# Fifteen decode steps in slots of their own, Wo prepared at other slots, and a narrower store of values

## The chip, the cores and the metric

One NeuronCore of one Trainium2 chip runs the kernel. It has five queues that work at once: TensorE (PE; its weight loads are shown as PEld), VectorE (DVE), ScalarE (ACT), GpSimd (POOL) and SyncE (SP), which only issues DMAs. The metric is the time of one execution on the device in microseconds; lower is better. A profile is taken of one execution, and shows each instruction with its start, its length and what ended the idle time before it.

## The reference

A transformer block over 2048 tokens of width 512, whose attention and MLP both read the same normalised input:

```
xn  = layernorm(x)                                  # [2048, 512]
q, k, v: 16 query heads, 4 key/value heads, 32 wide # Wq, Wkv
scores = q k^T / sqrt(32) + slope * (key - query)   # causal, ALiBi
attn = softmax(scores) v  ->  @ Wo + bo
W = LUT[4-bit codes] * scales, blocks of 32         # gate, up: 4096x512, down: 512x4096
mlp = down( gelu_tanh(gate(xn)) * up(xn) )
out = x + attn + mlp
```

The result is wanted close to float32. So most matrix products are made of fp16 pairs: an operand is split into a high and a low part, and three matmuls (high by high, high by low, low by high) stand for one.

## The kernel before, in words

A preamble (the first 112 us) normalises x, turns it, projects q, k and v and stores them in DRAM, and makes the scales and the first group's weights. Then come 16 groups; group i does the attention of head i and the MLP for hidden units 256 i to 256 i + 255, with all 2048 tokens. A tail adds x and the output projection.

**Slots.** A group has 48 slots, and each queue walks through them with its own program: in each slot TensorE does one piece of the MLP (six matmuls of gate, up or down, `PIECES`), and, where the table `PLAN` says so, one block of scores (a 128-row tile of queries by up to 512 keys, line 1370) and one unit of attention by values (line 1394). Heads begin 8 slots before their group. What an engine does in a slot is written out by hand in its `body`; an engine takes its instructions strictly in this order, waits for semaphores, and may so be some slots behind TensorE.

- TensorE: scores into a ring of four PSUM banks; gate and up; down, whose bank VectorE must have added to `acc` (line 1545) first.
- VectorE: maximum of each score block (1588, 1590), the shift for the softmax (1609), two steps of gelu (1554, 1561), the product with up (1569), its cast to fp16 (1577), the accumulation (1545), and the decoding.
- ScalarE: the exponentials (1475), their cast to the high fp16 half (1485, into a ring of four `pair` buffers, each free when its transpose has landed), square and tanh of gelu (1456, 1462), and `rows_hi` (389).
- GpSimd: low half of the probabilities (1734), low half of the MLP's product, `il` (1742), and `rows_lo` (393).
- SyncE: transposes of the probabilities by DMA (`turn`, 1203), q and k loads, gathering and storing of outputs, transposes of the weights (`turn_rows`, 399), and loads of the packed weights (`load_raw`, 352 and 357).

**Decoding the next weights.** While group i runs, the weights of group i + 1 are made, for the matrices m = 0, 1, 2 (gate, up, down), each in five instructions on VectorE (`decode_step`): shift the low code into place (366), the high code (369), mask both (373), and scale each half into `wf` (382, twice). One step stands in a slot: the rows of five begin at slots 8, 18 and 28 (`DECODE_FROM`). At the row's start + 5 ScalarE writes the fp16 high rows over the raw buffer, at + 6 GpSimd the low rows into a part of `o3`, at + 8 SyncE issues the two transposes, at + 11 the load of the raw weights of group i + 2 into the same buffer, which waits until the transposes have landed. The last group decodes nothing.

**Wo, in the last group (15).** `load_early` (SyncE, slot 12) brings Wo into the buffers of the decoding, by four DMAs, and a row of scales by a fifth. `wo_max` (VectorE, slots 17 to 20) takes its maxima and minima per partition, two reductions in each slot; `spread_tops` (SyncE, slot 27) writes the 128 maxima to DRAM, waits for that, and reads them back to all partitions; `wo_scale` (VectorE, slot 29) waits for it and makes the scale; ScalarE casts the high parts in slots 31 to 34 and VectorE makes the low parts a slot later. `load_x` (slot 41) waits for them.

**Values.** In the preamble, v is split into a high and a low half; the tile `vt` has four parts of 32 columns per head: high, ones, low, zeros. GpSimd fills ones and zeros by two memsets. `store_values` writes all four parts to `v_parts` in DRAM. At slot 0 of groups 0, 4, 8 and 12 `load_v` (1168) brings the high and the low part in with two DMAs, in runs of 64 bytes.

## Time and profile before

| | |
|---|---|
| median of 3 runs | 1640.24 us (1639.86 to 1642.94) |
| the profiled execution's own time | 1641.02 us |
| its span, first to last instruction | 1639.2 us |
| busy: TensorE / VectorE | 1429.3 us (87%) / 1297.4 us (79%) |
| busy: ScalarE / GpSimd | 975.9 us (60%) / 1000.8 us (61%) |
| mean granted TensorE clock | 0.977 |
| DMA queue of SyncE, share of 16 engines' span | 80.8% |

The busy times are shares of the whole span, preamble and tail included. In rows of a timeline the first number is the start in us from the span's start, the second the length; in square brackets stands how long the engine was idle before, and what ended that. A row of a timeline can merge several instructions (x4). `L382` is line 382 of the kernel. Matmul ends are modelled, so TensorE's idle time is a little less than what a stop costs.

### The profile page before, as it was taken

What the parts mean: (1) busy time and instruction counts of PE and PEld (TensorE: products, weight loads), DVE (VectorE), ACT (ScalarE), POOL (GpSimd) and SP (SyncE); (2) the same over time, 40 slices, a digit from 0 to 9 for tenths busy, and PEclk for the clock granted to TensorE, in tenths of its full rate; (3) what the DMA queues carried; (4) which work ended last, traced back from release to release, by engine and by line L of the source; (5) the groups of instructions that cost most, each with busy time, mean ns of one, the idle gap of its engine ahead of it and who ended that gap; (6) DMA issues with size and microseconds to landing.
All of it is one profiled execution on the core that took longest, in us unless ns stands there. A gap on an engine that the chain in (4) does not pass through costs nothing.

```text
span 1639.2 us, 28993 instructions
## 1 busy us (share of the span) xinstructions
PE 1429.3 (87%) x9281; PEld 684.1 (42%) x9281; DVE 1297.4 (79%) x2639; ACT 975.9 (60%) x2124; POOL 1000.8 (61%) x670
## 2 busy tenths in 40 slices
PE   5978998999889989889989989899888999897598
PEld 4743443444334434444434434344433444343243
DVE  8858787888868788888868788888868788875466
ACT  3347666666656666665666666666656666664330
POOL 3226676666656677666656666777656766774341
PEclk9979999999999999999999999999999999998799
DMA  7878969788897888798889879886998988887665
GB/s 219 231 176 175 171 119 170 149 161 154 160 163 144 160 155 165 145 152 149 166 158 153 157 151 160 147 174 136 173 154 154 153 158 153 147 152 133 120 155 198
DMA packets 784799, 260.97 MB, mean 159 GB/s; under 512 B 734512, under 2 KB 755896, under 8 KB 784392
## 3 DMA queue, kind: packets, MB, share of 16 engines
q1 hardware_dynamic: 780328, 253.48, 80.8%
q10 hardware_dynamic: 4320, 5.64, 1.0%
q8 instruction: 75, 1.23, 0.3%
q14 instruction: 76, 0.62, 0.1%
HBM read 52.30 MB, written 21.89 MB: 45 GB/s over the span
## 4 chain that ended last, share of the span: by engine, by line
DVE 30%; PE 18%; issue 14%; ACT 10%; DMA 10%; POOL 6%; SPq 4%; ACTq 0%; DVEq 0%; POOLq 0%
DMA pt<-pair 8%; PE up_ps L1348 5%; ACT p L1475 5%; POOL pair L1734 5%; DVE mxp L1588 4%; DVE acc L1545 4%; PE gate_ps L1348 4%; PE s_ps L1370 3%; DVE dec L369 3%; DVE wf L382 3%; DVE prod L1569 2%; PE down_ps L1326 2%; ACT gl L1456 2%; DVE s_ps L1590 2%; DVE dec L373 2%
## 5 line engine op out<-in xcount | busy, mean ns | idle before, releaser
L1734 POOL TENSOR_TENSOR pair<-p,pair 128x1024 f16<-128x1024 f32 (+7 forms) x384 | 615.2, 1610 | 347.3 <-ACT pair L1485 344.9
L1475 ACT ACTIVATE p<-s_ps,shift 128x512 f32<-128x512 f32 (+3 forms) x640 | 393.2, 619 | 222.6 <-DVE shift L1609 220.9
L1370 PE MATMUL s_ps<-kst,qst 128*128 128x512 f32 (+3 forms) x640 | 344.7, 540 | 115.2 <-ACT p L1475 106.9
L1485 ACT ACTIVATE pair<-p 128x1024 f16<-128x1024 f32 (+7 forms) x384 | 308.3, 808 | 100.4 <-DMA pt<-pair 97.3
L1588 DVE TENSOR_REDUCE mxp<-s_ps 128x1 f32<-128x512 f32 x384 | 260.2, 683 | 103.5 <-PE s_ps L1370 101.5
L1742 POOL TENSOR_TENSOR il<-prod,ih 128x512 f16<-128x512 f32 x128 | 156.2, 1220 | 149.7 <-DVE ih L1577 149.7
L1370 PEld LDWEIGHTS s_ps<-kst,qst 128*128 128x128 f32 x640 | 123.2, 193 | 233.6 <-ACT p L1475 157.9
L1326 PE MATMUL down_ps<-wh,ih 128*128 128x512 f16 x506 | 195.9, 387 | 28.2 <-DVE acc L1545 28.2
L1326 PE MATMUL down_ps<-wh,il 128*128 128x512 f16 x506 | 193.0, 381 | 16.0 <-POOL il L1742 16.0
L1348 PE MATMUL up_ps<-xh,wh 128*128 128x512 f16 x512 | 200.2, 391 | 0.0
L1348 PE MATMUL gate_ps<-xh,wh 128*128 128x512 f16 x512 | 197.6, 386 | 0.6 <-DVE gl L1561 0.6
L1348 PE MATMUL up_ps<-xh,wl 128*128 128x512 f16 x512 | 197.2, 385 | 0.0
L1348 PE MATMUL up_ps<-xl,wh 128*128 128x512 f16 x512 | 196.7, 384 | 0.0
L1348 PE MATMUL gate_ps<-xh,wl 128*128 128x512 f16 x512 | 194.7, 380 | 0.0
L1348 PE MATMUL gate_ps<-xl,wh 128*128 128x512 f16 x512 | 194.6, 380 | 0.0
L1326 PE MATMUL down_ps<-wl,ih 128*128 128x512 f16 x506 | 193.1, 382 | 0.0
L1545 DVE TENSOR_TENSOR acc<-down_ps,acc 128x512 f32<-128x512 f32 x237 | 161.3, 681 | 24.6 <-PE down_ps L1326 24.4
L1590 DVE CUSTOM_DVE_ANT_0 s_ps<-s_ps,mask_row 128x128 f32<-128x128 f32 (+3 forms) x256 | 125.5, 490 | 29.4 <-PE s_ps L1370 29.0
L1554 DVE SCALAR_TENSOR_TENSOR gl<-gl,gate_ps 128x512 f32<-128x512 f32 x128 | 87.5, 684 | 69.9 <-ACT gl L1456 66.5
L1394 PE MATMUL o_ps<-pt,vst 128*32 128x256 f16 (+1 forms) x3456 | 119.2, 272 | 27.0 <-DMA pt<-pair 17.0
L1456 ACT ACTIVATE gl<-gate_ps,cur 128x512 f32<-128x512 f32 x128 | 87.2, 682 | 69.3 <-PE gate_ps L1348 69.2
L1475 ACT ACTIVATION_READ_ACCUMULATOR p<-s_ps,shift 128x1 f32 x640 | 128.2, 200 | 0.0
(249 smaller groups left out, 2064.6 us busy)
## 6 DMA issues: line engine op xcount, KB each, us to landing
o<-oraw SPq DMA_DIRECT2D x256, 64.0 KB, 2.0
qst<-q_parts SPq DMA_DIRECT2D x192, 64.0 KB
q_parts<-o SPq DMA_DIRECT2D x24, 256.0 KB, 3.4
pt<-pair SPq DMA_TRANSPOSE x384, 4.3
raw<-L_ffn_gate_W_packed_dram SPq DMA_DIRECT2D x16, 256.0 KB, 3.1
raw<-n_L_ffn_up_W_packed_dram SPq DMA_DIRECT2D x16, 256.0 KB, 3.0
raw<-L_ffn_down_W_packed_dram SPq DMA_DIRECT2D x32, 128.0 KB, 2.6
o<-l_recips SPq DMA_DIRECT2D x64, 64.0 KB, 2.1
```

The lines of the kernel that those rows point to most:

```text
L1326: mm = nc.tensor.matmul(dst[:], lhs, rhs, start=(q == 0), stop=(q == 5))
L1348: mm = nc.tensor.matmul(dst[:], lhs, rhs, start=(q == 0), stop=(q == 11))
L1370: nc.tensor.matmul(s_ring[n % len(s_ring)][:, 0:cols], qst[:, c % 2, i4 * P:(i4 + 1) * P], kst[:, m * CH:m * CH + cols], start=True, stop= ...
L1394: mm = nc.tensor.matmul(dst if tok else dst.rearrange("p (a n) -> p a n", a=2), lhs, rhs, start=k < VPARTS, stop=k + VPARTS >= len(todo), ...
L1456: nc.scalar.activation(gl[a][:], gate_ps[:], ACT.Square, scale=cur[par][:, a:a + 1]).then_inc(square_done, 1)
L1475: nc.scalar.activation(p32[p % PR][:, at:at + cols], s_ring[n % len(s_ring)][:, 0:cols], ACT.Exp, bias=shift[t % len(shift)][:, 0:1], accu ...
L1485: nc.scalar.activation(pair[n % PH][:, 0:cols], p32[n % PR][:, 0:cols], ACT.Copy).then_inc(phi_done, 1)
L1545: nc.vector.tensor_tensor(acc[:, n % NT, :], bank[:], before, ALU.add).then_inc(acc_done, 1)
L1588: nc.vector.tensor_reduce(mxp[t % 2][:, m:m + 1], bank[:, 0:cols], AX.X, ALU.max).then_inc(red_done, 1)
L1590: nc.vector.tensor_tensor_reduce(bank[:, 0:cols], bank[:, 0:cols], mask_row[:, CH - cols:CH], 1.0, -3e38, ALU.add, ALU.max, mxp[t % 2][:, ...
L1734: nc.gpsimd.tensor_tensor(pair[n % PH][:, cols:2 * cols], p32[n % PR][:, 0:cols], pair[n % PH][:, 0:cols], ALU.subtract).then_inc(plo_done, 1)
L1742: nc.gpsimd.tensor_tensor(il[w % 2][:, a, :], prod[a][:], ih[w % 2][:, a, :], ALU.subtract).then_inc(il_done, 1)
```

## The change

Three things are changed; the arithmetic of the result is not.

1. The decode steps get slots one by one, listed for each matrix; what follows them keeps its distance from the last step (+ 1, + 2, + 4, + 7, as before).
2. In the last group, the load of Wo goes from slot 12 to slot 1, the maxima from 17 to 20 to 14, 16, 17 and 19; `spread_tops` is split into `store_tops` (slot 21) and the reading back (slot 28); the scale goes from 29 to 37, the casts from 31 to 34 to 38, 40, 42 and 43, the load of x from 41 to 46.
3. `vt` and `v_parts` have two parts for four; the memsets and the wait for them go, and `load_v` is one DMA. The first `load_raw(0, 1)` is issued ahead of the last store of values, not in slot 0.

```diff
-DECODE_FROM = (8, 18, 28)
-DECODE_AT = {s + step: (m, step) for m, s in enumerate(DECODE_FROM) for step in range(5)}
-ROWS_HI_AT = {s + 5: m for m, s in enumerate(DECODE_FROM)}
-ROWS_LO_AT = {s + 6: m for m, s in enumerate(DECODE_FROM)}
-TURN_ROWS_AT = {s + 8: m for m, s in enumerate(DECODE_FROM)}
-LOAD_RAW_AT = {s + 11: m for m, s in enumerate(DECODE_FROM)}
+DECODE_SLOTS = ((4, 7, 10, 13, 14), (16, 19, 22, 24, 25), (28, 31, 32, 34, 37))
+DECODE_AT = {s: (m, step) for m, slots in enumerate(DECODE_SLOTS) for step, s in enumerate(slots)}
+SCALES_READY_AT = DECODE_SLOTS[0][0]
+ROWS_HI_AT = {slots[-1] + 1: m for m, slots in enumerate(DECODE_SLOTS)}
+ROWS_LO_AT = {slots[-1] + 2: m for m, slots in enumerate(DECODE_SLOTS)}
+TURN_ROWS_AT = {slots[-1] + 4: m for m, slots in enumerate(DECODE_SLOTS)}
+LOAD_RAW_AT = {slots[-1] + 7: m for m, slots in enumerate(DECODE_SLOTS)}
-LOAD_EARLY_AT, LOAD_FULL_AT, SPREAD_TOPS_AT, LOAD_X_AT = 12, 25, 27, 41
+LOAD_EARLY_AT, LOAD_FULL_AT, STORE_TOPS_AT, SPREAD_TOPS_AT, LOAD_X_AT = 1, 25, 21, 28, 46
-WO_MAX_AT, WO_SCALE_AT, WO_HI_AT = (17, 18, 19, 20), 29, (31, 32, 33, 34)
+WO_MAX_AT, WO_SCALE_AT, WO_HI_AT = (14, 16, 17, 19), 37, (38, 40, 42, 43)
...
-    v_s = nc.dram_tensor("v_parts", [KVH, P, NT, 4 * HD], F16, kind="Internal").ap()
+    v_s = nc.dram_tensor("v_parts", [KVH, P, NT, 2 * HD], F16, kind="Internal").ap()
...
-                nc.gpsimd.memset(vt[:, :, :, 1, :], 1.0).then_inc(vt_filled, 1)
-                nc.gpsimd.memset(vt[:, :, :, 3, :], 0.0).then_inc(vt_filled, 1)
...
-                    for part in range(2):
-                        sp.dma_start(vst[:, :, part * HD:(part + 1) * HD],
-                                     v_s[i // REP, :, :, 2 * part * HD:(2 * part + 1) * HD]).then_inc(v_in, 16)
+                    sp.dma_start(vst[:], v_s[i // REP]).then_inc(v_in, 16)
...
+                sp.wait_ge(w_in[0], 16 * W_DMAS)
+                load_raw(sp, 0, 1)
                 store_values(sp, NCH - 1)
...
-                    for m in range(3):
+                    for m in (1, 2):
...
-                def spread_tops():
+                def store_tops():
 
                     sp.wait_ge(wtop_done, 1)
                     sp.dma_start(w_s.rearrange("(p o) -> p o", o=1), wtop).then_inc(wtop_out, 16)
+
+                def spread_tops():
+
                     sp.wait_ge(wtop_out, 16)
...
-                        if s == DECODE_FROM[0]:
+                        if s == SCALES_READY_AT:
```

## Rows read from the trace of the kernel before

**Rows 1.** Stretches: busy us (x instructions) of each engine, granted clock, DMA share, GB/s.

```profile
658.30:690.70 32.40, 28.59 (x181) 12.59 (x179) 25.64 (x53) 20.55 (x46) 22.50 (x15) 1.00 0.82 145
1470.60:1498.40 27.80, 27.80 (x181) 12.60 (x179) 21.24 (x49) 21.04 (x48) 19.19 (x14) 1.00 0.77 135
1212.40:1215.70 3.30, 3.30 (x9) 1.11 (x7) 1.20 (x3) 0.00 (x0) 1.27 (x1) 0.52 0.86 162
296.60:1470.60 1174.00, 1051.94 (x7089) 483.75 (x7087) 963.30 (x1964) 758.27 (x1664) 791.83 (x522) 0.99 0.85 155
```

**Rows 2.** TensorE's waits, groups 2 to 14: us in total, times, longest.

```profile
PE s_ps L1370 <- ACT p L1475: 87.6, 80, 2.0
PE down_ps L1326 <- POOL il L1742: 13.7, 13, 1.1
PE o_ps L1394 <- DMA vst<-v_parts: 9.8, 3, 3.6
```

**Rows 3.** Timeline of TensorE in group 6: start, length in us, [idle before, releaser].

```profile
680.53 0.49 PE L1370 MATMUL s_ps<-kst,qst 128*128 128x512 f32 x1 [0.84 <-ACT p L1475]
...
689.22 0.49 PE L1370 MATMUL s_ps<-kst,qst 128*128 128x512 f32 x1 [1.69 <-ACT p L1475]
...
694.65 0.51 PE L1370 MATMUL s_ps<-kst,qst 128*128 128x512 f32 x1 [0.54 <-ACT p L1475]
...
703.29 0.49 PE L1370 MATMUL s_ps<-kst,qst 128*128 128x512 f32 x1 [1.59 <-ACT p L1475]
...
721.46 0.50 PE L1370 MATMUL s_ps<-kst,qst 128*128 128x512 f32 x1 [1.49 <-ACT p L1475]
```

**Rows 4.** Timeline of VectorE in group 6.

```profile
683.99 2.54 DVE L382 TENSOR_TENSOR wf<-dec,sc 128x512 f32<-128x512 f16 x1
```

**Rows 5.** Timeline of ScalarE in group 6.

```profile
686.57 1.06 ACT L389 ACTIVATE raw<-wf 128x1024 f16<-128x1024 f32 x1 [4.01 <-DVE wf L382]
```

**Rows 6.** Timeline of VectorE in group 15.

```profile
1513.79 0.69 DVE L1661 TENSOR_REDUCE sc<-wf 128x1 f32<-128x512 f32 x1 [12.15 <-DMA dec<-in_L_attn_Wo_dram]
...
1553.18 0.29 DVE L1671 TENSOR_REDUCE sc<-sc 128x1 f32<-128x128 f32 x1 [16.16 <-DMA sc<-wo_tops]
```

**Rows 7.** Timeline of SyncE's issues in group 15.

```profile
1499.78 1.30 SPq L1285 DMA_DIRECT2D wf<-in_L_attn_Wo_dram  x2
```

**Rows 8.** DMA issues, groups 2 to 14: count, KB each, median us to landing.

```profile
raw<-L_ffn_gate_W_packed_dram SPq DMA_DIRECT2D x12, 256.0 KB, 3.1
...
vst<-v_parts SPq DMA_DIRECT2D x6, 128.0 KB, 4.2
```

**Rows 9.** VectorE's decode instructions, groups 2 to 14: busy us, mean ns | idle before.

```profile
L382 DVE TENSOR_TENSOR wf<-dec,sc 128x512 f32<-128x512 f16 x78 | 78.5, 1020 | 0.0
...
L373 DVE TENSOR_SCALAR dec<-dec 128x1024 int32<-128x1024 int32 x39 | 48.2, 1237 | 0.0
L369 DVE TENSOR_SCALAR dec<-raw 128x512 int32<-128x512 int32 x39 | 42.2, 1082 | 0.0
...
L366 DVE TENSOR_SCALAR dec<-raw 128x512 int32<-128x512 int32 x39 | 28.9, 742 | 0.0
```

**Rows 10.** Timeline of SyncE's issues in group 6.

```profile
663.49 1.36 SPq L1203 DMA_TRANSPOSE pt<-pair  x1
...
715.61 1.32 SPq L399 DMA_TRANSPOSE wl<-o  x1
718.51 0.40 SPq L352 DMA_DIRECT2D raw<-n_L_ffn_up_W_packed_dram  x1
...
732.00 1.58 SPq L399 DMA_TRANSPOSE wh<-raw  x1
733.63 1.33 SPq L399 DMA_TRANSPOSE wl<-o  x1
...
738.73 0.94 SPq L357 DMA_DIRECT2D raw<-L_ffn_down_W_packed_dram  x2
```

**Rows 11.** Chain of waits, the longest pieces of 660 to 760: start, us.

```profile
746.16 4.11 DMA pt<-pair
```

More of the change, by code:

```diff
@@ L408, in storing_steps @@
         e[n] for n in ("q_s", "k_s", "aug_s", "qst", "kst", "p_out", "q_in", "k_in", "k_last"))
-    vt = wh[1][:, 0:2].rearrange("p m a n -> p (m a n)").rearrange("p (j g a d) -> p j g a d", j=TPC, g=KVH, a=4)
+    vt = wh[1][:, 0].rearrange("p a n -> p (a n)").rearrange("p (j g a d) -> p j g a d", j=TPC, g=KVH, a=2)
     orows = acc[:, NT - 1, OROWS_AT:OROWS_AT + P]
@@ L539, in preamble @@
         vscale_done = sem("vscale_done")
-        vt_filled = sem("vt_filled")
         os_turned = sem("os_turned")
@@ L572, in store_v @@
                     sp.wait_ge(v_lo, c + 1)
-                    if c == 0:
-                        sp.wait_ge(vt_filled, 2)
                     store_values(sp, c)
@@ L921, in values_lo @@
                     nc.vector.scalar_tensor_tensor(
-                        vt[:, :, :, 2, :].rearrange("p j g d -> p (j g) d"), vps[:].rearrange("p (n d) -> p n d", d=HD),
+                        vt[:, :, :, 1, :].rearrange("p j g d -> p (j g) d"), vps[:].rearrange("p (n d) -> p n d", d=HD),
                         vscale[:, 0:1], vt[:, :, :, 0, :].rearrange("p j g d -> p (j g) d"), ALU.mult, ALU.subtract
@@ L1245, in body @@
                                 load_full(sp, 0)
+                            if s == STORE_TOPS_AT:
+                                store_tops()
                             if s == SPREAD_TOPS_AT:
@@ L1376, in values @@
                         if u == 0:
-                            pe.wait_ge(v_in, (h // REP + 1) * 32)
+                            pe.wait_ge(v_in, (h // REP + 1) * 16)
                         for n in range(max(last - PH + 1, 0), last + 1):
```

## The prediction

> **What bounds the kernel now.** I read the page's first two parts, then the chain of waits, the waits of TensorE, the timelines of one head group, and the last group by itself. The page puts TensorE at 87% busy, VectorE at 79%. A group (one head of attention beside one sixteenth of the MLP, 48 slots) takes 90.3 us: 1174 us for groups 2 to 14, thirteen of them [rows 1]. No engine is full, so what counts is what stops TensorE. Over those thirteen groups it waited 87.6 us for exponentials on ScalarE, 13.7 us for `il` from GpSimd and 9.8 us for the values, three times [rows 2].
>
> Where the waits for exponentials fall is seen in group 6: 0.84 and 1.69 us behind the first row of decode steps (slots 8 to 12), 0.54 and 1.59 behind the second, 1.49 behind the third [rows 3]. The chain there: the fifth step of the first row took 2.54 us on VectorE [rows 4] at a place where the scores' maxima were due; ScalarE stood 4.01 us before the copy to fp16 rows that needs this step [rows 5], with a gelu square and the next exponentials queued behind; then TensorE found no free score bank. The third row's rows_lo on GpSimd (slot 34) delays `il`, needed at slot 38.
>
> The last group is the control: it decodes nothing. Its first 17 slots are the same 181 matmuls as in group 6, in 27.8 us with TensorE busy throughout, against 32.4 us [rows 1]. Its later part is worse: VectorE stood 12.15 us for Wo and 16.16 us for the broadcast of Wo's maxima [rows 6], and TensorE behind it, since accumulate and the score maxima share that queue.
>
> **Part 1, Wo in group 15.** The load now leaves at SyncE's slot 1, the first maximum is taken at slot 14; before, slots 12 and 17. SyncE runs behind the others there: slot 12's load was issued at 1499.78 [rows 7], when VectorE was already at slot 17, and landed at 1513.8 (the row of 12.15 us). From slot 1, issued near 1480, it should land near 1494, and slot 14 starts at 1494. That wait shrinks to 0 to 3 us. The broadcast gets nine slots (28 to 37) in place of two, some 15 us, its store leaves seven slots ahead of it: that wait goes. 12.15 + 16.16 = 28.3. After each of the two stops TensorE ran some 3 us at half its clock, near 2 us more each: 32 us. Against it: the five DMAs take 5 us of the queue (from 1499.78, [rows 7], to 1504.7) ahead of the transposes of probabilities, in a stretch where it has nothing to spare. It can cost TensorE 0 to 5; I take 2. The Wo reductions and casts are the same instructions; in 38 to 44 the casts stand before the last pairs on ScalarE, but the present 2.75 us wait at slot 47, which has the same source, is caused at 31 to 34; I leave it equal. `load_x(0)` at 46 stays behind the same transposes. Gain 30 (20 to 35).
>
> **Part 2, values.** One load of 256 KB in 2 KB runs for two of 128 KB in 64 B runs, and a smaller store. TensorE waited 9.8 us for it over groups 4, 8 and 12 [rows 2], and each wait is followed, as in group 12, by 3.3 us at granted clock 0.52 (1.2 GHz) for nine matmuls, some 1.3 us lost [rows 1]. The second load was issued 0.7 to 1.4 us after the first and landed 4.2 us later; a 256 KB load of raw weights lands in 3.1 us [rows 8]. So the wait falls by some 2 us, and part of the slow clock goes: 3 us each, 9 in all (3 to 14). The two memsets dropped from GpSimd stood ahead of a wait for ScalarE's first cast: nothing. The early `load_raw(0, 1)` puts one issue (0.6 us) ahead of the last store of values, and load_v gives one back: nothing, within 1 us either side.
>
> **Part 3, the decode steps, groups 0 to 14.** What the rows cost: in group 6, 0.84 + 1.69, 0.54 + 1.59, 1.49 plus 1.05 (13.7 over 13) for `il`, 7.2 us of idle; six stops, and each loses about 0.24 us more, since idle is counted from a matmul's modelled end and not from where the next would have started. 8.6 us. The comparison of 32.4 with 27.8 agrees: 4.6, of which the wait at slot 2, not from decode, and its restart are some 1.5.
>
> No instruction is added or dropped: per matrix 0.742 + 1.082 + 1.237 + 2 x 1.020 = 5.1 us [rows 9], 15.3 per group, now in slots where VectorE has little else (7, 13, 22, 37 have almost nothing). VectorE is then never five slots in arrears: its lag behind TensorE, up to 6.0 us at slots 12, 15 and 21 now, should stay under 4.5, where I find no stop now. But slots 10 to 19 hold about as much VectorE work as TensorE work (16 us each), so what remains of a lag doesn't drain there. I take two thirds of the 8.6: 5.7. Bounds: nothing, and all of it.
>
> What is moved with them: rows_hi, rows_lo, the transposes and the next raw load go from slots 13, 14, 16, 19 to 15, 16, 18, 21; from 23, 24, 26, 29 to 26, 27, 29, 32; from 33, 34, 36, 39 to 38, 39, 41, 44. On GpSimd the third rows_lo (2.1 us) leaves the place ahead of `il`, and comes behind the last pairs of the head and before `il` of slot 41, needed only at slot 2: hidden. On ScalarE it joins output_hi at 38, one us, and 40 is empty. SyncE is the tight one. From 663.49 to 753.09 in group 6 (76 issues, the first in [rows 10]) it was issuing or stepping between issues in all but 7 of 90 us, so a group can't fall below some 84 us unless the issues get shorter. The third matrix's two transposes (1.58 + 1.33) and its raw load (0.94) [rows 10] now come after the transposes of the head's last pairs, which helps slot 47 a little, and amid the first ones of the next head. Its raw load must wait for transposes that left just before: as the second's does now, 716.9 to 718.51, 1.6 us [rows 10]; between 41 and 44 there is only the store of outputs and one transpose. The turns of slots 45 to 47 go some 2.5 us later, that of 44 by 0.8. That place is on the chain of waits: 4.11 us at 746.16 [rows 11]. Cost 0.8 to 5.5 (all three issues and the wait); I take 1.5, since the turn of 44 is the one on the chain. Net 4.2 per group, x 15 = 63 us. Bounds: -1.5 x 15 and, by the SyncE floor of 84, 6.3 x 15 = 95.
>
> **Sum.** The profiled execution took 1641.0 us, 1.8 outside its span of 1639.2. 1641.0 - 30 - 9 - 63 = 1539. The median of the runs is 0.8 below it: 1538.
>
> **A rule that speaks against part 3.** The fifth step took 2.54 us where the mean of its kind is 1.02 [rows 4, 9], and the time lies inside the instruction. The Trainium skill (SBUF — State Buffer, on the shared port pair) says that VectorE instructions with two SBUF inputs or in a two-port mode, and GpSimd instructions, take one lock for their whole length, and the other blocks fully. The trace agrees as far as one row can. If fifteen lone steps each meet a GpSimd instruction, every one pays, and spreading buys nothing; this is the second rival, priced below from rows.
>
> **Rivals.**
> (a) SyncE keeps pace and nearly all decode stops go: 6.3 to 8.6 per group. 1641 - 39 - 95 = 1507, at the end 1480. For: in group 15 without decode there was no stop at all in 17 slots. Against: there rows and raw loads were absent from SyncE as well.
> (b) The stops only move, through long steps in new places: 15 x 0 to 15 x 1.5 gained. 1602 to 1580, say 1595. VectorE is at 963.3 / 13 = 74 us of 90 per group [rows 1]; three more long steps (1.5 us over the mean each) make 78.6, still under the group, so it would cost the gain and no more. For: fewer steps in a row means more meetings. Against: GpSimd was as busy before, 792 of 1174 us [rows 1].
> (c) Slower than before: the wrap from slot 41 to slot 2. If the three issues and the wait, 1.58 + 1.33 + 0.94 + 1.6 = 5.5 us, land in full on the first transposes of the next head, ScalarE's ring of four pairs stops exponentials at slots 47 to 2 every group. It is decided at 39 / 15 = 2.6 us per group over the decode gain: with a gain of 1.5 and a cost of 5.5, 1641 - 39 + 15 x 4 = 1662. For: the chain passes there already. Against: no turn but slot 44's is on it, and that one goes ahead of the raw load.
> (d) It doesn't do what it says: VectorE's slots are not light because its lag carries over from before; the time is that of (b).
>
> **Chances.** Forecast (1515 to 1570) 0.53, (a) 0.17, (b) with (d) 0.22, (c) 0.06, no change 0.02. The range, 1505 to 1600, takes in the bounds of parts 1 and 2, most of (b) and the near end of (a). This kernel's runs tell 0.2%, some 3 us, from no change. Faster 0.92, same 0.02, slower 0.06.
>
> **What would show it.** Group 15 near 88 us in place of 117, VectorE's waits for Wo and `wo_tops` under 3 us; `vst` waits near 1 us each; groups of 86 us; waits at slots 12, 16, 19, 23, 33 mostly gone, `il` no longer a releaser of down; the wait at slot 2 grown to about 3 us; SyncE idle under 3 us per group. Wrong would be: new waits for exponentials at slots 17 to 26 or 35 to 41, or groups still over 89 us.

## The result

| | before | after |
|---|---|---|
| median | 1638.97 us (1635.6 to 1644.05, 19 runs) | 1629.88 us (1627.09 to 1640.63, 19 runs) |
| ratio | | 0.995, 95% interval 0.9937 to 0.9962 |
| span of the profiled execution | 1639.2 us | 1626.6 us |
| groups 0 to 14, mean of one | 90.56 us | 90.56 us |
| group 15 | 117.6 us | 103.6 us |
| preamble / tail | 112.1 / 51.0 us | 114.7 / 49.9 us |

Faster by 0.4 to 0.6%, some 8 us, where 1538 us with a range of 1505 to 1600 was predicted (6%). The fifteen groups that decode are as long as before, to the hundredth; all that was gained lies in the last. (A group's length is the distance between the first matmuls of two groups, in the profiled execution.)

The page of the kernel after, busy us of each engine:

```profile
PE 1443.6 (89%) x9281; PEld 693.7 (43%) x9281; DVE 1273.6 (78%) x2639; ACT 978.3 (60%) x2124; POOL 1018.7 (63%) x668
```

Stretches of the kernel after, groups 2 to 14 and group 15; the columns are those of [rows 1]:

```profile
296.60:1473.10 1176.50, 1064.93 (x7087) 492.17 (x7086) 937.24 (x1964) 760.81 (x1664) 809.02 (x520) 0.98 0.81 155
1473.10:1576.70 103.60, 83.70 (x540) 38.04 (x539) 66.02 (x140) 54.06 (x114) 51.65 (x34) 0.92 0.80 146
```

TensorE's waits in the kernel after, groups 2 to 14, as in [rows 2]:

```profile
PE s_ps L1371 <- ACT p L1476: 71.0, 64, 3.4
PE o_ps L1395 <- DMA pt<-pair: 22.1, 16, 2.4
PE gate_ps L1349 <- DVE gl L1562: 12.8, 11, 1.4
PE o_ps L1395 <- DMA vst<-v_parts: 5.5, 3, 2.5
```

The waits for exponentials fell by 16.6 us only, `il` is gone and the values cost half. But transposes that came late grew from 7.3 to 22.1 us, and the second gelu step (12.8 us, none before) is new. The longest wait for exponentials grew from 2.0 to 3.4 us: fewer waits, longer ones. The clock took a share as well: in groups 2 to 14 the same matmuls kept TensorE busy for 1064.9 us at a granted clock of 0.98, against 1051.9 at 0.99 in [rows 1], one us more per group. A large piece lies behind the stops of slot 28, here in group 6 (columns as in [rows 1]):

```profile
711.00:714.00 3.00, 2.90 (x41) 1.68 (x42) 0.04 (x1) 1.44 (x2) 1.29 (x1) 0.73 1.33 164
```

TensorE in group 6 (657.1 to 748.3 us) of the kernel after, to be held against [rows 3]:

```profile
662.61 0.50 PE L1371 MATMUL s_ps<-kst,qst 128*128 128x512 f32 x1 [2.14 <-ACT p L1476]
...
682.60 0.81 PE L1395 MATMUL o_ps<-pt,vst 128*32 128x256 f16 x24 [0.82 <-DMA pt<-pair]
...
707.85 0.50 PE L1371 MATMUL s_ps<-kst,qst 128*128 128x512 f32 x1 [1.48 <-ACT p L1476]
...
711.10 1.14 PE L1395 MATMUL o_ps<-pt,vst 128*32 128x256 f16 x36 [2.08 <-DMA pt<-pair]
...
736.71 0.39 PE L1349 MATMUL gate_ps<-xh,wh 128*128 128x512 f16 x1 [1.36 <-DVE gl L1562]
...
745.45 0.39 PE L1371 MATMUL s_ps<-kst,qst 128*128 128x256 f32 x1 [1.27 <-ACT p L1476]
```

The stops of [rows 3] are gone; these stand at slots 2, 13, 28 (two), 42 and 47. Counted over groups 2 to 14, as the excess of the distance between two matmuls over what it is where nothing waits (this is my sum over TensorE's records, not a view; it takes in matmuls at the slow clock, and another choice of the distance without a wait moves a row by some tenths, the sums by some 2 us), per group. "The wrap" is the passage from the last slots of a group to the first of the next:

| stop at slot | before, us | after, us | what ends it |
|---|---|---|---|
| 12, 16, 19, 23, 33, 38 | 8.62 | 1.41 | VectorE behind a row of decode steps |
| 28, 29: values, up, down | 0 | 3.05 | a transpose that landed late |
| 28: scores | 0.55 | 1.83 | exponentials behind a late tanh |
| 2: scores, down | 1.18 | 2.86 | exponentials; the wrap |
| 42: gate | 0 | 1.12 | gelu, ScalarE |
| 47: scores and values | 0.57 | 1.58 | exponentials |
| all stops | 12.56 | 12.98 | |

So the mechanism of part 3 did what was said of it, 7.2 us per group (5.7 predicted); and 7.6 us came in other places. The places of the largest are seen in group 6.

**SyncE, slots 21 to 28.** Its issues in the kernel after:

```profile
704.32 1.86 SPq L1199 DMA_TRANSPOSE pt<-pair  x1
706.22 1.06 SPq L353 DMA_DIRECT2D raw<-L_ffn_gate_W_packed_dram  x1
707.34 5.66 SPq L1199 DMA_TRANSPOSE pt<-pair  x3
```

The transpose issued at 707.34 is the one whose values TensorE needs at slot 28; it lands at 710.97 (3.63 us on the chain), and TensorE goes on at 711.10. It wasn't the data that was late: over groups 2 to 14 this transpose's input lay ready 6.9 us before the issue, 5.6 in the kernel before (these and the next are my medians over the records of GpSimd, SyncE and TensorE). The load of the first matrix's raw weights, 1.06 us, stands ahead of it on the queue, but it did so in the kernel before too:

```profile
700.10 0.58 SPq L352 DMA_DIRECT2D raw<-L_ffn_gate_W_packed_dram  x1
700.73 0.36 SPq L1178 DMA_DIRECT2D qst<-aug_rows  x1
701.14 1.23 SPq L1180 DMA_DIRECT2D qst<-q_parts  x3
702.47 3.89 SPq L1203 DMA_TRANSPOSE pt<-pair  x2
```

Two things are new. SyncE is late from the wrap on, where the third matrix's issues now stand: counted from the group's start, the transpose of slot 3 is issued at 12.2 us for 9.7 before, and that of slot 22, the one in question, at 50.2 for 47.5. (At slots 17 and 18 it is level with before for a moment, as the first matrix's two transposes now stand behind these and not ahead.) And TensorE comes to slot 28 sooner, at 50.9 us for 52.5. Before, the transpose landed at 51.0, ahead of TensorE; now it lands at 54.1, three us behind.

**VectorE and ScalarE, slots 25 to 28.** VectorE in the kernel after:

```profile
702.21 0.68 DVE L383 TENSOR_TENSOR wf<-dec,sc 128x512 f32<-128x512 f16 x1
...
703.41 2.02 DVE L383 TENSOR_TENSOR wf<-dec,sc 128x512 f32<-128x512 f16 x1
...
705.70 0.68 DVE L1555 SCALAR_TENSOR_TENSOR gl<-gl,gate_ps 128x512 f32<-128x512 f32 x1
```

ScalarE there:

```profile
705.47 1.06 ACT L390 ACTIVATE raw<-wf 128x1024 f16<-128x1024 f32 x1 [1.09 <-DVE wf L383]
706.43 0.71 ACT L1463 ACTIVATE gl<-gl,cur 128x512 f32<-128x512 f32 x1
707.04 0.67 ACT L1476 ACTIVATE p<-s_ps,shift 128x512 f32<-128x512 f32 x1
```

The second matrix's fifth step takes 2.02 us in slot 25. The gelu step behind it, then the tanh on ScalarE, then the exponentials stand in one line, and TensorE waits for these until 707.85. There are two suspects in that line: the decode step, and the high row (L390) that waits for it.

Why the step is long is in the trace. GpSimd's instruction that was running when it began:

```profile
702.30 2.58 POOL L1735 TENSOR_TENSOR pair<-p,pair 128x1024 f16<-128x1024 f32 x1
```

It ends at 704.88, the step 0.55 us later. So does every long one: of the 78 scaling steps of groups 2 to 14, 37 took over 0.9 us, all 37 began while a GpSimd instruction ran, and all ended 0.55 to 0.56 us after its end. In the kernel before there were 13 long ones, by the same rule. The change made nearly three times as many.

**GpSimd, slots 38 to 42** in the kernel after (L335 is the output's low part, L394 the third matrix's low row):

```profile
737.49 1.17 POOL L335 TENSOR_TENSOR o<-o 128x512 f16<-128x512 f32 x1
738.60 2.33 POOL L1735 TENSOR_TENSOR pair<-p,pair 128x1024 f16<-128x1024 f32 x1
740.89 2.13 POOL L394 TENSOR_TENSOR o<-wf,raw 128x1024 f16<-128x1024 f32 x1
742.99 1.15 POOL L1743 TENSOR_TENSOR il<-prod,ih 128x512 f16<-128x512 f32 x1
```

The change put the third matrix's rows at 38 and 39, where the output's steps stood already. The same meeting is on ScalarE. The rows are read here as the suspects for slots 42 and 47; e6 and e11 below try it.

**Group 15.** VectorE's list of waits there names neither Wo nor the maxima any more. In their place, on SyncE of the kernel after:

```profile
1483.96 1.26 SPq L1283 DMA_DIRECT2D wf<-in_L_attn_Wo_dram  x2
1485.27 1.33 SPq L1283 DMA_DIRECT2D dec<-in_L_attn_Wo_dram  x2
1486.64 2.42 SPq L1284 DMA_DIRECT2D raw<-column_scales  x1
1489.18 10.47 SPq L1199 DMA_TRANSPOSE pt<-pair  x2
```

And on TensorE:

```profile
1500.36 1.15 PE L1395 MATMUL o_ps<-pt,vst 128*32 128x256 f16 x18 [9.52 <-DMA pt<-pair]
```

SyncE's record of two transposes lasts 10.47 us right behind Wo's load, where that of two at 695.93 in group 6 lasts 3.74, and TensorE stands 9.52 us for them.

### The profile page after: what moved, and what is told of

It reads as the page before. It is cut to its first block, busy times and chain, and to the rows that moved or that the text cites. A ratio compares the mean times of both kernels' runs of the same rounds, so it can differ in the third digit from the quotient of the medians.

```text
span 1626.6 us, 28986 instructions
## 1 busy us (share of the span) xinstructions
PE 1443.6 (89%) x9281; PEld 693.7 (43%) x9281; DVE 1273.6 (78%) x2639; ACT 978.3 (60%) x2124; POOL 1018.7 (63%) x668
## 4 chain that ended last, share of the span: by engine, by line
PE 25%; DVE 20%; POOL 14%; issue 13%; DMA 9%; ACT 8%; SPq 4%; ACTq 0%; DVEq 0%; POOLq 0%
POOL pair L1735 10%; DMA pt<-pair 8%; PE up_ps L1349 6%; PE gate_ps L1349 5%; PE down_ps L1327 5%; DVE mxp L1589 5%; DVE acc L1546 3%; PE o_ps L1395 3%; ACT p L1476 3%; PE s_ps L1371 3%; POOL il L1743 2%; DVE prod L1570 2%; SPq L1199 2%; DVE s_ps L1591 2%; DVE wf L383 2%
## 5 line engine op out<-in xcount | busy, mean ns | idle before, releaser
L1735 POOL TENSOR_TENSOR pair<-p,pair 128x1024 f16<-128x1024 f32 (+7 forms) x384 | 640.2, 1678 | 325.2 <-ACT pair L1486 324.9
L1349 PE MATMUL gate_ps<-xh,wh 128*128 128x512 f16 x512 | 197.4, 386 | 12.8 <-DVE gl L1562 12.8
L1395 PE MATMUL o_ps<-pt,vst 128*32 128x256 f16 (+1 forms) x3456 | 126.3, 283 | 48.6 <-DMA pt<-pair 42.8
L1562 DVE SCALAR_TENSOR_TENSOR gl<-gl,gate_ps 128x512 f32<-128x512 f32 x128 | 87.3, 682 | 66.2 <-ACT gl L1463 65.8
L1555 DVE SCALAR_TENSOR_TENSOR gl<-gl,gate_ps 128x512 f32<-128x512 f32 x128 | 87.3, 682 | 65.2 <-ACT gl L1457 63.4
```

What stands on the lines that cost most here:

```text
L1349: mm = nc.tensor.matmul(dst[:], lhs, rhs, start=(q == 0), stop=(q == 11))
L1395: mm = nc.tensor.matmul(dst if tok else dst.rearrange("p (a n) -> p a n", a=2), lhs, rhs, start=k < VPARTS, stop=k + VPARTS >= len(todo), ...
L1555: nc.vector.scalar_tensor_tensor(gl[a][:], gl[a][:], 1.0, gate_ps[:], ALU.add, ALU.mult).then_inc(inner_done, 1)
L1735: nc.gpsimd.tensor_tensor(pair[n % PH][:, cols:2 * cols], p32[n % PR][:, 0:cols], pair[n % PH][:, 0:cols], ALU.subtract).then_inc(plo_done, 1)
```

## The experiments

Medians are of 4 to 9 runs each; the kernel before, run beside them, gave medians of 1636 to 1639 us. Theory S: SyncE's queue of issues. Theory P: the pile-up of the output's and the third matrix's rows. Theory D: Wo's bytes on the DMA engines. Theory Q: the decode step of slot 25. Where an expectation gives one of these letters another sense, it says so.

### Each part alone: e1, e2, e10

Each is the kernel before with one part of the diff shown ahead of the prediction: e1 with the lines from `DECODE_SLOTS` to `LOAD_RAW_AT`, e2 with the Wo slots and `store_tops`, e10 with the narrow values and the moved first load. The first line of each:

```diff
 # e1
+DECODE_SLOTS = ((4, 7, 10, 13, 14), (16, 19, 22, 24, 25), (28, 31, 32, 34, 37))
 # e2
+WO_MAX_AT, WO_SCALE_AT, WO_HI_AT = (14, 16, 17, 19), 37, (38, 40, 42, 43)
 # e10
+    v_s = nc.dram_tensor("v_parts", [KVH, P, NT, 2 * HD], F16, kind="Internal").ap()
```

> The kernel before with part 3 alone: the fifteen decode steps and what follows them in the new slots. Theory S (SyncE's queue is the floor of a group: the decode stops went, and the same microseconds came back as waits for transposes and pair buffers): groups stay at 90.6 us within 0.7, waits of TensorE for exponentials at slots 12, 16, 23, 33 gone, new ones at 28, 42 and 47; 1639 within 8. Theory V (part 3 gained its 60 us and the two other parts lost it): groups near 87 us, 1585.

> The kernel before with part 1 alone: Wo's load at slot 1, maxima, scale and casts at the new slots. Theory S: group 15 has its two stops of 12 and 16 us no more, but the five DMAs put ahead of the transposes stop TensorE some 10 us near slot 9; group 15 from 117 to about 104 us, whole 1626 (-13). My forecast of before said 2 us for that stop and -30: 1609.

> The kernel before and the values' part of the change alone (values without their constant columns, one load each, the first raw load moved). The prediction gave this part 9 us: 1628 to 1632 us. Theory S (SyncE's queue holds the stream by the group's sum of issues, and the values' loads save one issue in four groups): almost nothing of it comes through, 1634 to 1640 us; the waits for the values fall from 9.8 to about 5 us, and come back elsewhere.

| | median us | ratio to before | 95% interval | in us |
|---|---|---|---|---|
| e1, decode slots | 1653.63 | 1.0101 | 1.0071 to 1.0131 | +17 |
| e2, Wo | 1627.46 | 0.9933 | 0.9904 to 0.9961 | -11 |
| e10, values | 1628.59 | 0.9943 | 0.992 to 0.9965 | -9 |
| all three | 1629.88 | 0.995 | 0.9937 to 0.9962 | -8 |

(The last column is the ratio minus 1, times 1639.) The parts add up to -3, with intervals of 4 to 5 us on each: with the whole they agree. Values brought what was predicted, 9 (6 to 13), and theory S's own expectation for it, next to nothing, failed. Wo brought 11 for 30. The decode slots by themselves made the kernel slower, for 63 faster. In e1's trace groups 0 to 14 take 91.3 us each, 0.7 more than before, 11 us in sum; another 3 us lie in the preamble, which e1 doesn't touch.

### SyncE relieved: e3 and e5

```diff
+ACT_STORE_RECIPS_AT, ACT_SPREAD_RECIPS_AT = 6, 17
+ACT_RAW_AT = {25: (0, 2), 36: (1, 2), 10: (2, 1)}
...
-                            if s in LOAD_RAW_AT and i + 2 < HEADS:
...
+                        if s in ACT_RAW_AT and i >= 0:
+                            m, ahead = ACT_RAW_AT[s]
...
+                                load_raw(act, m, g)
```

The DMAs of raw weights (four) and of reciprocals (eight), twelve of some 77 a group, leave from ScalarE instead of SyncE, with the waits that stood before them, and in other slots; the bytes are the same. (e5's expectation counts six and six; it is four and eight.) e3 does it to the changed kernel, e5 to the kernel before.

> The changed kernel, with 12 of SyncE's 76 issues per group (raw weight loads, storing and spreading of the reciprocals) issued from ScalarE's queue in slots where it has little (6, 10, 17, 25, 36). Same DMAs, same bytes. Theory S: SyncE gets some 6 us back per group, the waits at slots 2 and 28 shrink by over half, groups fall by 3 us or more: 1585 or less. Rival D (the DMA engines themselves, 85% busy, are the floor, not the issuing): transposes land as late as now, groups within 1 us of 90.6, 1630. Rival P (GpSimd and ScalarE at slots 38 and 39 set it): waits at 42 and 47 stay, groups fall by 1 to 2 us at most.

> The kernel before, and of SyncE's issues twelve a group (six loads of raw rows, six stores and spreads of reciprocals) made by ScalarE instead; decode rows, Wo and values as before. It asks whether the relief needs the new slots. Theory S (two limits lie one behind the other: with the rows of five the decode clusters hold back the stream, with single slots SyncE's queue does): the clusters still stop TensorE at slots 16, 23 and 33, SyncE is less late than there, little comes back: 1625 to 1640 us, the stops before the block and values matmuls that name a transpose's DMA going but no more than 1 us per group. Rival (SyncE's queue alone set the group's length, whatever the slots): the group shortens by some 2.7 us as it did with the single slots, and the time is 1590 to 1600 us.

e3: 1584.83 us, ratio 0.9685 (0.9658 to 0.9711), 45 us under the changed kernel. The late transposes of slot 28 are gone. TensorE's waits of e3, groups 2 to 14:

```profile
PE s_ps L1365 <- ACT p L1470: 69.5, 65, 3.1
PE gate_ps L1343 <- DVE gl L1566: 15.0, 13, 1.4
PE o_ps L1389 <- DMA vst<-v_parts: 2.1, 3, 1.2
PE o_ps L1389 <- DMA pt<-pair: 1.8, 2, 1.0
```

`pt<-pair` went from 22.1 to 1.8 us and the two rows that theory S does not speak of stayed. The sum of SyncE's issue records went from 78.4 to 72.6 us per group, the group from 90.5 to 87.7. The same bytes alone don't rule the DMA engines out, since e3 also moves the twelve DMAs in time. The transposes' own records do: from a transpose's input being ready to its issue it took 3.2 us in the kernel after and 1.5 in e3, from its issue to its landing 4.1 and 4.3 (my means over the 312 transposes of groups 2 to 14). The time was lost ahead of the issue, in the queue, and not in the engines. Whether fewer issues or fewer waits in the queue brought more is not separated.

e5: 1614.38 us, ratio 0.9867 (0.9845 to 0.9889), 22 us under before, between the two expectations. So SyncE cost the kernel before some 20 us too, which TensorE's waits for transposes (7.3 us) had not shown; with the single slots it cost twice that. The stops at 16, 23 and 33 are in e5 what they were (2.02, 1.94, 1.84 us per group).

### The output's steps apart from the third rows: e6 and e11

```diff
-OUTPUT_HI_AT, OUTPUT_LO_AT = 38, 39
+OUTPUT_HI_AT, OUTPUT_LO_AT = 36, 37
```

> The changed kernel with ScalarE's twelve issues as in e3, and the output's high and low steps at slots 36 and 37 instead of 38 and 39. Theory P (the stops at slots 42 and 47, 1.3 and 1.6 us per group in e3, come of output_hi, rows_hi, the power and the exponential all lying in slot 38 on ScalarE, and output_lo, rows_lo in 39 on GpSimd): both stops shrink to under 0.5 us, the group from 87.85 to 85.5 to 86.5 us, and the time is 1550 to 1565 us. Rival D (the stops come of the block's own work at those slots, or of DMA traffic): nothing moves, 1582 to 1588 us.

> The changed kernel, and the output's high and low steps at slots 36 and 37 instead of 38 and 39, with all twelve issues still on SyncE. Behind the relief the same edit took 31 us (e3 to e6). If the group's length is SyncE's queue (theory S), the stops at 42 and 47 go here too, but their time comes back as longer waits for the transposes: 1615 to 1630 us. If the two limits only add up, each with its own price, it is 1595 to 1602 us.

e6: 1553.82 us, ratio 0.9498 (0.9479 to 0.9516), 31 us under e3. The stop at 47 went from 1.61 us per group to 0, that at 42 from 1.31 to 0.73, that at 2 from 2.51 to 1.88; one of 1.11 came at 44, where down waits for VectorE. TensorE's waits of e6, groups 2 to 14:

```profile
PE s_ps L1365 <- ACT p L1470: 44.3, 52, 2.3
PE down_ps L1321 <- DVE acc L1550: 12.3, 13, 1.0
PE gate_ps L1343 <- DVE gl L1566: 7.6, 12, 0.8
```

e11, the same edit with all issues on SyncE: 1610.74 us, ratio 0.9836 (0.9809 to 0.9862), 19 us under the changed kernel, more than theory S allowed and less than the 31 us behind the relief. The late transposes stayed (21.1 us for 22.1). So each of the two limits has a price of its own, 45 and 19 us, and together they bring 76, 12 more than the sum.

### What the decode slots are worth then: e13

> The kernel before with both of e6's additions (ScalarE's twelve issues, output steps at 36 and 37), but rows of five, Wo and values as before. It measures what the decode slots are worth where nothing else is late. If the prediction's mechanism was right and only its gain was eaten by the two limits, this kernel stays near e5, at 1608 to 1622 us, since the stops at 16, 23 and 33 are still VectorE's clusters; e6 is then some 60 us faster, of which 21 are Wo and values as measured alone, and the rest, 35 to 40 us, is the decode slots' (predicted: 63). Rival (the gain of e6 is the relief's and the output's own, whatever the slots): 1575 to 1585 us.

1610.01 us, ratio 0.9825 (0.9806 to 0.9843). With rows of five, both additions brought 29 us; with single slots 76. TensorE's waits of the whole e13:

```profile
PE s_ps L1364 <- ACT p L1469: 98.7, 91, 3.5
PE down_ps L1320 <- DVE acc L1549: 23.5, 3, 13.9
PE down_ps L1320 <- POOL il L1746: 16.9, 15, 1.1
```

The stops at 16, 23 and 33, behind the rows of five, are there as in [rows 3], 2.0, 1.8 and 1.8 us per group. e6 against e13 is a ratio of 0.9498 / 0.9825 = 0.967, 54 us; less the 20 of Wo and values, 34 for the decode slots, with some 7 either way from the intervals of the four ratios. By the same sum their worth is 10 us with SyncE relieved alone (0.9685 / 0.9867: 30 less 20, some 8 either way), and -17 with nothing relieved (5 either way). This is the main finding: one edit, three prices, by what stands behind it. That the prices of Wo and values are the same in all three settings is taken over, not measured. The lengths of groups 0 to 14 in the traces, in which Wo has no part, say the same: less the 12.6 us that values bring there in e10, the decode slots are worth -11 us (e1), 9 (89.30 in e5, 87.85 in e3) and 31 (89.00 in e13, 86.09 in e6).

### The stop at slot 28: e7, e9, e12

```diff
 # e7: the rows wait some slots
-ROWS_HI_AT = {slots[-1] + 1: m for m, slots in enumerate(DECODE_SLOTS)}
+ROWS_HI_AT = {15: 0, 30: 1, 40: 2}
 # e9
-DECODE_SLOTS = ((4, 7, 10, 13, 14), (16, 19, 22, 24, 25), (28, 31, 32, 34, 37))
+DECODE_SLOTS = ((4, 7, 10, 13, 14), (16, 19, 20, 22, 24), (28, 31, 32, 34, 37))
 # e12
+DECODE_SLOTS = ((4, 7, 10, 13, 14), (16, 19, 22, 24, 28), (31, 32, 34, 37, 39))
```

> As e6, and each matrix's row steps wait a few slots after its last decode step (high 15, 30, 40; low 16, 31, 42; turn 18, 33, 44), so that the high row's step on ScalarE isn't held by a decode step just ahead of it. Theory P: the stop of 1.83 us before the block matmuls of slot 28 (there ScalarE's power waits behind the high row of slot 26, which waits for VectorE's long decode step of slot 25) goes to under 0.6 us, and the wrap's stop at slot 2 (2.5 us) to under 1.5 us, since the third row is done within the group: 2 us per group less than e6, 1520 to 1540 us. Rival (the stop at 28 is the decode step itself on VectorE, not the row behind it): within 5 us of e6.

> As e6, and the second matrix's decode steps at slots 16, 19, 20, 22 and 24 instead of 16, 19, 22, 24 and 25. In e7 the row steps were taken away from slot 26 and the stop before slot 28's block matmuls stayed 1.82 us. Theory Q (the stop comes of the decode step itself: in slot 25 it lasts 2 us on VectorE, the gate's inner step of slot 26 starts behind it, ScalarE's tanh of slot 27 waits for that, the two exponentials wait behind the tanh, and the block matmuls of slot 28 for the exponentials): the stop falls to 0.5 to 0.8 us, 1.1 us per group, 1534 to 1543 us. Rival (the other work of slots 24 to 26 holds it, or a decode step at slot 20 takes its place): the time stays at 1550 to 1556 us, or a new stop of the same size shows at slots 21 to 24.

> As e6, and the second matrix's last decode step at slot 28 instead of 25, the third's five at 31, 32, 34, 37 and 39 instead of 28, 31, 32, 34 and 37 (in e6's trace VectorE idles 1.5 us in slot 28 and 1.1 in slot 39). Theory Q (the step in slot 25 makes the stop at slot 28, and e9 lost its gain only to the steps packed at 20 and 22): the stop at slot 28 falls from 1.83 to about 0.5 us, nothing new of that size comes, 16 us per run less than e6: 1532 to 1542 us. Rival (VectorE is so full from slot 16 to 37 that any place of the fifteen steps costs the same): a stop moves to slot 31, 33 or 42, 1550 to 1560 us.

e7, e9 and e12 all stand on e6. e7: 1561.6 us, ratio 0.955 (0.9533 to 0.9566), 8 us slower than e6. The stop at 28 stayed at 1.82 us per group with the row out of the way, so it was not the row. The stop at 2 went from 1.88 to 0.63, and 0.6 and 0.99 came at 4 and 9: nothing won.

e9: 1588.59 us, ratio 0.9692 (0.9665 to 0.9719). The stop at 28 fell to 0.89, so it was the decode step; but 2.76 and 0.66 us came at slots 23 and 24, behind the steps packed at 20 and 22, and the kernel is 32 us slower than e6 by the ratios. Moving three decode steps by one or two slots each cost four times what the whole change had won.

e12: 1552.28 us, ratio 0.9472 (0.945 to 0.9494), the fastest, though not told apart from e6. TensorE of e12 at slot 28 of group 6:

```profile
680.91 0.49 PE L1365 MATMUL s_ps<-kst,qst 128*128 128x512 f32 x1 [0.20 <-ACT p L1470]
```

VectorE of e12 just before:

```profile
678.14 0.43 DVE L1595 CUSTOM_DVE_ANT_0 s_ps<-s_ps,mask_row 128x256 f32<-128x256 f32 x1 [0.31 <-PE s_ps L1365]
```

The stop there is 0.55 in place of 1.83, as theory Q had it, and VectorE even waits for work. Of the 16 us per run expected from that, 1.5 came: the stop at 42 (0.73) went as well, but those at 2, 3, 4, 9 and 28 (values) grew by 1.7 us per group in sum, and all stops went from 7.77 to 7.50.

### Wo: e4, e8, e14

e4 issues Wo's five DMAs from ScalarE at slot 3. e8 is e7 with Wo's four loads at slots 43 and 47 of group 14 and at 3 and 8 of group 15. e14 is the changed kernel with half of Wo's bytes: it leaves out the load of Wo's last 256 columns, so their part of the result is not computed from Wo.

```diff
 # e4, on ScalarE
+                        if i == LAST and s == 3:
+                            load_early(act)
 # e8, per (group, slot): which part of Wo, the last the row of scales
+WO_LOADS = {(LAST - 1, 43): 2, (LAST - 1, 47): 3, (LAST, 3): 0, (LAST, 8): 1, (LAST, 28): KVH}
 # e14
-sp.dma_start(wo[g], Wo.rearrange("(r g d) n -> g r d n", r=REP, g=KVH)[g]).then_inc(wo_in, 16)
+sp.dma_start(wo[g][:, 0:C // 2], Wo.rearrange("(r g d) n -> g r d n", r=REP, g=KVH)[g][:, :, 0:C // 2]).then_inc(wo_in, 16)
```

> The changed kernel, with the five DMAs of Wo's load issued by ScalarE at slot 3 of group 15 and not by SyncE at slot 1. Theory Q (they held the transposes because they stood ahead in the same queue): the 10 us stop near slot 9 is 0 to 3 us, 1622. Rival D (1.25 MB ahead of the transposes in the DMA engines, whoever issues): a stop of 6 to 10 us stays, 1629.

> As e7, and Wo's four loads spread out on SyncE: two in the last slots of group 14 (43, 47), two in group 15 (slots 3 and 8), the column at slot 28. Theory D (the stop of 10 us at slot 9 of the last group is the transposes' DMAs queued behind Wo's 1.25 MB on the DMA engines, so it shrinks when they never lie together): the stop falls to under 4 us, the time is 6 to 9 us under e7. Rival: the loads, wherever they lie, delay the transposes by the same sum, and the time is within 2 us of e7.

> The changed kernel, but Wo's four loads at slot 1 bring the first 256 of 512 columns alone (0.5 MB instead of 1 MB; the other half of Wo isn't computed with the right numbers). Theory D (the transposes' DMAs share the DMA engines with the load's bytes): the stop before slot 9's values matmuls falls from 10.3 to 5 to 6 us, 4 to 5 us less in the run than the changed kernel's 1629.9. Rival (a transpose issued behind five bulk copies pays a fixed price, a drain or a change of mode, whatever their size): the stop stays at 9.5 us or more, and so does the time.

e4: 1629.74 us, ratio 0.9951 (0.992 to 0.9981), the changed kernel's. Stops of 3.6, 1.3 and 4.7 us at slots 6, 7 and 9 for one of 10.3. SyncE of e4, while Wo's loads are issued by ScalarE from 1487.3 to 1493.4:

```profile
1489.88 14.32 SPq L1209 DMA_TRANSPOSE pt<-pair  x2
```

No load of Wo is ahead of these two on SyncE's queue. Of the 14.32 us some 1.6 are a wait for the second's input; the two issues themselves last 4.92 and 7.81 us, and the first transpose lands 16.3 us after its issue (10.9 in the kernel after, 4.4 at 695.93 in group 6).

e8: 1560.97 us, ratio 0.9545 (0.953 to 0.956), e7's. The stop at 9 fell from 11.4 to 1.0, and 4.7 at slot 2, 3.6 at 9 (scores) and others came; group 15's stops are 20.8 in sum for 20.7. Theory D expected 6 to 9 us less: spreading moved the price and didn't lower it, as the rival had it.

e14: 1624.5 us, ratio 0.9925 (0.9896 to 0.9953). SyncE of e14 in group 15:

```profile
1483.81 7.01 SPq L1199 DMA_TRANSPOSE pt<-pair  x2
```

TensorE of e14 there:

```profile
1491.21 0.67 PE L1395 MATMUL o_ps<-pt,vst 128*32 128x256 f16 x18 [2.53 <-DMA pt<-pair]
```

Half the bytes: the first transpose lands 7.2 us after its issue, for 10.9, the stop fell from 10.3 to 2.6 us (another, 1.95, came at slot 13), and the group's stops from 27.5 to 22.7. The median is 5.4 us lower, but the intervals of the two ratios overlap, so the verdict rests on one trace of each. There a fixed price is ruled out: it would have left a stop of 9.5 us or more. The bytes count, as theory D has it; that it is by sharing the DMA engines, and not in some other way, is argued.

## Why the prediction was wrong, step by step

**Part 1, Wo: 30 predicted, 11 (6 to 16) measured.** That both waits of VectorE in [rows 6] go was right. The step that failed is "It can cost TensorE 0 to 5; I take 2". I priced the five DMAs by their place in the queue, 5 us, and not by their bytes. In e2 the stop at slot 9 is 10.1 us, and 3.2 and 2.9 came at slots 44 and 28: group 15's stops fell from 41.1 to 23.4 us, by 18 and not by 30. (The trace of e2 is of an execution of 1620.7 us, where the median is 1627.5; the 18 are its, the 11 are the medians'.)

**Part 2, values: 9 predicted, 9 (6 to 13) measured.** The three waits fell from 9.8 to 6.1 us in e10, so 3.7 and not 6 came from the wait itself; where the rest came from isn't settled.

**Part 3: 63 predicted, 17 slower (12 to 21) measured alone.** The sum's first term held: 7.2 of 8.6 us per group went, for 5.7. The failed step is its counter-term, "Cost 0.8 to 5.5 (all three issues and the wait); I take 1.5, since the turn of 44 is the one on the chain": what came is 7.6 us per group. Three things were wrong in it:
- SyncE was looked at at the wrap only, and its lateness was taken to end there. It is 2.7 us later than before at slot 22 too, and TensorE comes to slot 28 earlier than before: 3.05 us per group at slots 28 and 29, and 1.7 at slot 2. e3 shows that the queue is the cause; that the third matrix's issues make it late, and not the other moves, is read from the order of issues and not tried by a run of its own.
- "On ScalarE it joins output_hi at 38, one us, and 40 is empty": the sum of what stands there is right and the order isn't looked at. The tanh of the gate and the low rows on GpSimd lie behind. e11 shows 19 us for moving the output's two steps by two slots, e6 31 us behind the relief.
- "its lag ... should stay under 4.5, where I find no stop now": a mean lag says nothing of what an individual long step holds up. 1.28 us per group at slot 28, shown by e9 and e12.

Of the 7.6 us about one is the clock, in these same places; the prediction has no term for it in part 3 beyond the 0.24 us of a restart.

The range left out its own worst case. With a gain of nothing and a cost of 5.5 the text's terms allow -5.5 us per group, where the bounds say -1.5; and the upper end of 1600 leaves even -1.5 out, while slower had a chance of 0.06. The upper end of rival (a) is a slip: 8.6 x 15 = 129, and 1641 - 39 - 129 is 1473, not 1480. The floor of 84 us per group from SyncE was never reached and so isn't tested: with all issues on SyncE the shortest mean is e11's 89.5, and e6, at 86.1, has six us fewer of them. That SyncE is the tight queue was right; it costs by being late at single places, long before its sum is the group.

**Of the rivals,** (b), stops only move, is the one that came about. Its cause, long steps in new places, is real, but makes only the 1.28 us per group at slot 28 of the 7.6. VectorE's decode instructions of the kernel after, groups 2 to 14, against [rows 9]:

```profile
L383 DVE TENSOR_TENSOR wf<-dec,sc 128x512 f32<-128x512 f16 x78 | 105.2, 1349 | 0.0
...
L374 DVE TENSOR_SCALAR dec<-dec 128x1024 int32<-128x1024 int32 x39 | 40.2, 1032 | 0.0
...
L367 DVE TENSOR_SCALAR dec<-raw 128x512 int32<-128x512 int32 x39 | 16.2, 416 | 0.0
```

The scaling steps grew from 1020 to 1349 ns and the first from 742 shrank to 416: a matrix now takes 0.416 + 1.093 + 1.032 + 2 x 1.349 = 5.24 us for 5.10 (1.093 is the second step's mean in the same view). The Trainium skill (SBUF — State Buffer, on the shared port pair) says that of such a VectorE instruction and a GpSimd instruction the one that starts first has the ports for its whole length, and that the other blocks fully. The trace agrees: all 37 long scaling steps began inside a GpSimd instruction and ended 0.55 to 0.56 us behind its end. What didn't follow is the prediction's "every one pays": 41 of the 78 scaling steps stayed short, and in sum a matrix pays less than 3% more. (c), slower through the wrap, is right in sign for part 3 alone, and the lateness does come from the wrap, but slot 2 gives only 1.7 of the 7.6 us per group and the most is paid at slots 28 and 29.

**Beside part 3 stands a rule** that bears on e3 and e4. The Trainium skill (DMA: Bandwidth & Descriptors, Issuing engines are not separate DMA queues) says that DMAs of any issuing engine run on the same sixteen DMA engines, and that issuing from several saves only the issuer's time, "which is usually small relative to the DMA itself". Both halves agree with the traces: in e4 another issuer left Wo's price as it was, and a plain DMA takes 0.57 us of SyncE against 1.7 to 3.6 us from issue to landing. But small for one DMA isn't small for the queue. In sum the issues take 78.4 of 90.5 us, and in e3 twelve of them moved, 5.8 us of the issuer's time per group with the same bytes, brought 45 us.

## What to carry to other kernels

When work is moved off a late engine in a kernel in which no engine is full, ask which queue is second and how much of the time it takes back, and price every queue's order at the new place, not its sum: here one edit was worth -17, +10 or +34 us, by whether two other limits stood. Follow a queue that the edit makes late through the whole loop, not only to the end of the place where it becomes late. Relieve the second queue first, or try both together; moving ten or so issues to another queue is a cheap trial of whether the issuing queue is the limit, and the time from a DMA's input being ready to its issue, held against that from issue to landing, says the same from one trace. Here a bulk load beside a stream of transposes that TensorE waits for cost by its bytes at each of the places and queues tried.

## What the runs showed of the hardware that was not expected

- SyncE's queue limits by its issues: in the kernel after, 24 transposes of probabilities of 1.77 us mean, six of weights of 1.45 and 47 plain DMAs of 0.57 are 78 us of a 90.5 us group. That limit hardly shows as TensorE's waits (7.3 us for transposes before) where another engine is late as well: relief brought 22 us. It showed in ScalarE's waits for a free pair buffer, 62.8 us in groups 2 to 14 before.
- SyncE's record of two transposes behind 1.25 MB of bulk loads (1 MB of Wo and a row of scales spread to 128 partitions) lasts 10.47 us, behind 0.75 MB 7.01 us, and elsewhere, as in group 6, 3.74. With the 1.25 MB issued by ScalarE meanwhile the two issues last 4.92 and 7.81 us.
- The same scaling step of 128x512 on VectorE lasts from 0.68 to 2.65 us in one group of the kernel after. The long ones are those that begin while GpSimd works, and they end 0.55 us behind its instruction: 13 of 78 in groups 2 to 14 before, 37 after, 52 in e6. e6 has the most long steps and is 76 us faster than the kernel after, so their number by itself says little of the time.
- In the kernel after and the nine built on it the preamble is the same, and its end moved between 111.5 and 114.9 us: traces of one execution each can't tell 3 us apart.
